# Attention rewritten: a maxima-only rows pass, softmax sums by matmuls of ones, sixteen half-groups over a ring of five score banks

## What is computed

```python
q = (query @ Wq).reshape(bsz, tgt_len, 2 * H, D)      # H = 16, D = 16; k alike, v: H heads of 2 * D
q = apply_rotary_emb = apply_rotary_interleaved(q, cos, sin)
q1, q2 = (q[:, :, :, 0], q[:, :, :, 1])
attn1 = causal_attn_pair(q1, k1, v1, v2, mask, scale)  # softmax(q1 k1^T) v, float32
attn2 = causal_attn_pair(q2, k2, v1, v2, mask, scale)
f1 = jnp.fft.rfft(attn1, axis=1)
f2 = jnp.fft.rfft(attn2, axis=1)
attn_freq = f1 - lambda_full * f2
attn_freq = attn_freq * filt[None, :, None, None]
attn = jnp.fft.irfft(attn_freq, n=tgt_len, axis=1)
attn = attn * jax.lax.rsqrt(jnp.mean(attn * attn, axis=-1, keepdims=True) + EPS) * rms_weight
return attn.reshape(bsz, tgt_len, H * 2 * D) @ Wout
```

## Time and profile before

| | |
|---|---|
| time, median of 3 runs | 1559.61 us (1551.4 to 1561.73) |
| the profiled execution, span | 1553.8 us |
| normalise and what leads to attention's first scores | 0 to 133 us |
| attention, first 16 rows units alone | 133 to 171.7 us |
| attention, rows and probs together, to the last values | 171.7 to about 1014 us |
| end of attention, start of `middle` | 1014 to 1098 us |
| `middle` and `last` | 1098 to 1553 us |
| busy over the span | PE 1252.6, DVE 855.8, ACT 809.2, POOL 590.6 us |

### The profile page before, as it was taken

The page is one execution under the profiler, slowest core; times in us unless marked ns, Lnnn a source line. Parts: engine busy times, 40 slices in busy tenths (PEclk is TensorE's granted clock), DMA queues, the critical chain, the costliest instruction groups (busy, mean ns, idle before and its releaser), DMA issues. The chain is left out here.

```text
span 1553.8 us, 21592 instructions
## 1 busy us (share of the span) xinstructions
PE 1252.6 (81%) x6637; PEld 639.4 (41%) x6652; DVE 855.8 (55%) x1502; ACT 809.2 (52%) x1741; POOL 590.6 (38%) x662
## 2 busy tenths in 40 slices
PE   6854898798897897898998888956798888775985
PEld 4622233333443433334334323324566555542543
DVE  6554544834835635635636438145777655542886
ACT  2304577877887876877877888822121111110211
POOL 4433407146244252262361301200566655672121
PEclk9985789989899898998899799887999998997998
DMA  4364711802604505306207002013122111113330
GB/s 144 117 139 73 117 16 42 109 16 68 84 16 86 68 35 94 40 35 101 32 34 116 17 22 89 16 36 102 62 81 69 62 62 48 41 41 100 110 107 36
DMA packets 69358, 104.16 MB, mean 67 GB/s; under 512 B 8448, under 2 KB 34688, under 8 KB 69248
## 3 DMA queue, kind: packets, MB, share of 16 engines
q1 hardware_dynamic: 57472, 69.26, 22.9%
q0 software_dynamic: 7168, 25.17, 4.5%
q10 hardware_dynamic: 4608, 8.39, 1.4%
HBM read 68.85 MB, written 33.95 MB: 66 GB/s over the span
## 5 line engine op out<-in xcount | busy, mean ns | idle before, releaser
L1058 ACT ACTIVATE score<-score,nmax 128x1024 f32<-128x1024 f32 (+7 forms) x512 | 364.8, 713 | 165.7 <-DVE nmax L934 83.8
L1088 ACT ACTIVATE prob<-score 128x1024 f32<-128x1024 f32 (+3 forms) x384 | 297.7, 812 | 39.7 <-PE score L795 24.4
L776 PE MATMUL score<-kst,qst 96*128 96x512 bf16 (+3 forms) x768 | 222.8, 370 | 93.1 <-ACT score L1058 73.2
L937 DVE TENSOR_REDUCE nmax<-score 128x1 f32<-128x640 f32 (+3 forms) x256 | 250.7, 1020 | 80.3 <-PE score L780 77.4
L934 DVE TENSOR_REDUCE nmax<-score 128x2 f32<-128x256 f32 (+3 forms) x128 | 105.3, 825 | 243.5 <-PE score L780 243.5
L791 PE MATMUL score<-qst,kst 99*128 99x512 bf16 (+3 forms) x768 | 217.9, 354 | 24.4 <-ACT score L1058 10.3
L720 PE MATMUL misc<-xnT,wg 128*128 128x512 f32 x256 | 139.6, 644 | 24.4 <-DVE raw L874 16.7
L776 PEld LDWEIGHTS score<-kst,qst 96*128 96x128 bf16 x768 | 64.3, 104 | 219.9 <-ACT score L1058 143.7
L791 PEld LDWEIGHTS score<-qst,kst 99*128 99x128 bf16 x768 | 74.3, 103 | 191.6 <-ACT prob L1088 67.7
L780 PE MATMUL score<-mask_s,identb 128*128 128x128 bf16 x512 | 117.1, 238 | 0.0
L1131 POOL TENSOR_TENSOR sq<-y 128x512 f32<-128x512 f32 x14 | 14.5, 1034 | 255.5 <-DVE y L897 196.0
(11 more groups left out here) (229 smaller groups left out, 2168.2 us busy)
## 6 DMA issues: line engine op xcount, KB each, us to landing
piece_scratch<-pieces POOLq DMA_DIRECT2D x16, 768.0 KB, 4.1
qst<-piece_scratch SPq DMA_DIRECT2D x48, 256.0 KB, 9.6
kst<-piece_scratch SPq DMA_DIRECT2D x48, 256.0 KB, 18.9
x1in<-in_query SPq DMA_DIRECT2D x16, 256.0 KB, 2.7
v_scratch<-v ACTq DMA_DIRECT2D x16, 256.0 KB, 2.0
vg<-v_scratch SPq DMA_DIRECT2D x8, 512.0 KB, 15.7
att_scratch<-y SPq DMA_DIRECT2D x8, 512.0 KB, 2.7
m_aT<-att_scratch SPq DMA_DIRECT2D x16, 256.0 KB, 2.9
```

The source lines that it names most:

```text
L776: mm = nc.tensor.matmul(score[slot][:, bank, 0:w], qst[0:PIECES, g.slot, pair + k, i * P:(i + 1) * P], kst[0:PIECES, g.slot, pair + k, c0: ...
L937: nc.vector.tensor_reduce(nmax[:, pair, i:i + 1], src[:].rearrange("p a b -> p (a b)")[:, 0:(i + 1) * P], AX.X, ALU.max, negate=True).then ...
L1058: ins = nc.scalar.activation(s, s, ACT.Exp, bias=nmax[:, pair + k, i:i + 1], accum_out=den[:, pair + k, i:i + 1])
L1088: nc.scalar.activation(prob[:, u % NPROB, :, t0:HALF], score[slot][:, :, t0:HALF], ACT.Exp).then_inc(s_exp, 1)
```

## The change

**Half-groups.** The 8 groups of 8 pairs become 16 sets of 4 (one map of 4 heads each, `SETS`); `qst` and `kst` hold four sets. `stack` issues 12 transfers of half the size per set.

**Rows pass.** A unit now fills one bank of 512 columns. There are 38 per set. Short ones hold 4 or 2 heads with one mask matmul over all. DVE takes the maxima (L839 in the new file, 608 reduces in all, 384 before); ACT does nothing in this pass, and a rows unit gives back its bank after the maximum. For queries 512 and up a row's maxima come in two parts, joined by one minimum. The shift is the maximum alone, in two bfloat16 pieces: a probs matmul has 98 rows.

**Probs pass and sums.** A probs unit is one head in one bank: 768 exps of up to 512 columns instead of 384 of up to 1024. For every `values` event PE now also multiplies the same probabilities by `ones` into a new bank `den`, 4 more float32 matmuls. So there are 192 events as before, each of 8 float32 matmuls instead of 4. After each half ACT turns `den` into its reciprocal (Ln, then Exp with scale -1, `norm`), and DVE multiplies `acc` by it (`output`); in odd sets it also multiplies by minus lambda and adds to `oT`. POOL no longer scales the values.

**Order and waits.** One written-out list (`schedule`) with no hardware loop: the 38 rows units of set 0 stand alone, then each set's 48 probs units are merged with the next set's rows units; the last set's stand alone. `values` stands four units behind its probs, `norm` three units later and `out` six. The score ring has five single banks. The first values of a half wait for `norm`'s first read of `den` and for `out` to have read `acc`. The work on `misc` (projections, low-pass, shift transposes) is otherwise the same.

```diff
+SETS = 2 * B * G
+RING = 5
+NPROB = 12
+PROD = 6 * D
+ROWS = PROD + 2
...
+        for c0 in range(0, (i + 1) * P, HALF):
+            width = min(HALF, (i + 1) * P - c0)
+            n = max(1, HALF // width) if width != 384 else 1
+            units += [(i, c0, width, h, n) for h in range(0, GH, n)]
...
-    return [(h, j, w, g) for h in range(2) for j in range((h + 1) * TB // 2) for w in range(2) for g in (0, 2)]
...
+    return [(h, j, head) for h in range(2) for j in range((h + 1) * TB // 2) for head in range(GH)]
...
+def schedule():
+    units, start = [], []
+    units += [("rows", 0, u) for u in range(NRU)]
+    for n in range(SETS):
+        start.append(len(units))
+        mine = [("probs", n, m) for m in range(NPU)]
+        ahead = [("rows", n + 1, u) for u in range(NRU)] if n + 1 < SETS else []
+        units += merge(mine, ahead)
+    start.append(len(units))
...
+        for v in range(NV):
+            k = at["probs", n, v * GH + GH - 1] + VALUES_LATER
+            put(k, ("values", n, v))
+            if v in (NV // 3 - 1, NV - 1):
+                h = int(v == NV - 1)
+                put(k + NORM_LATER, ("norm", n, h))
+                put(k + OUT_LATER, ("out", n, h))
...
-        score = [ctx.enter_context(nc.psum_tensor(f"score{i}", [P, 2, HALF], F32)) for i in range(NSLOT)]
+        score = [ctx.enter_context(nc.psum_tensor(f"score{i}", [P, HALF], F32)) for i in range(RING)]
         acc = ctx.enter_context(nc.psum_tensor("acc", [P, HALF], F32))
+        den = ctx.enter_context(nc.psum_tensor("den", [P, HALF], F32))
         misc = ctx.enter_context(nc.psum_tensor("misc", [P, HALF], F32))
         miscb = misc[:].bitcast(BF16)
...
+            def slot_free(k):
+                if k >= RING:
+                    kind, count = done[k - RING]
+                    pe.wait_ge(s_max if kind == "rows" else s_exp, count)
...
+            def rows(n, u):
+                i, c0, width, first, heads = RU[u]
+                k = place["rows", n, u]
+                slot_free(k)
+                bank = score[k % RING][:, 0:heads * width].rearrange("p (a s) -> p a s", a=heads)
+                for x in range(heads):
+                    mm = nc.tensor.matmul(bank[:, x], qst[0:PROD, n % 4, first + x, i * P:(i + 1) * P],
+                                          kst[0:PROD, n % 4, first + x, c0:c0 + width], start=(x == 0),
+                                          stop=(x == heads - 1), skip_group_check=True)
+                if c0 + width == (i + 1) * P:
+                    mask = mask_s[:].rearrange("p (o s) -> p o s", o=1).broadcast_to([P, heads, P])
+                    mm = nc.tensor.matmul(bank[:, :, width - P:width], identb[:], mask, start=False, stop=True,
+                                          skip_group_check=True)
+                mm.then_inc(s_unit, 1)
...
-            def values(g, m):
...
-                if j == 0 and which == 0:
-                    if g.reg is not None or g.c > 0 or h:
-                        pe.wait_ge(s_oT, g.times(2, h))
-                end = j == (h + 1) * TB // 2 - 1 and which == 1
-                for head in range(GH):
-                    pslot = (m - 1 + head // 2) % NPROB
-                    v = (vg, vn)[which]
-                    mm = nc.tensor.matmul(acc[head * 32:head * 32 + 32, t0:HALF],
-                                          v[:, g.slot, j, head * 32:head * 32 + 32],
-                                          prob[:, pslot, head % 2, t0:HALF],
-                                          start=(j == 0 and which == 0), stop=end, skip_group_check=True)
+            def values(n, v):
+                h, j, _ = PU[v * GH]
+                pe.wait_ge(s_exp, probs_done(n, v * GH + GH - 1))
                 t0 = max(j * P - h * HALF, 0)
+                if j == 0 and 2 * n + h > 0:
+                    pe.wait_ge(s_den, 2 * n + h)
+                    pe.wait_ge(s_acc, 2 * n + h)
+                end = j == (h + 1) * TB // 2 - 1
+                for total, bank in enumerate((acc, den)):
+                    for head in range(GH):
+                        x = slice(head * 2 * D, (head + 1) * 2 * D)
+                        mm = nc.tensor.matmul(bank[x, t0:HALF], ones[:] if total else vg[:, n // 2 % 2, j, x],
+                                              prob[:, (n * NPU + v * GH + head) % NPROB, t0:HALF],
+                                              start=(j == 0), stop=end, skip_group_check=True)
                 mm.then_inc(s_pv, 1)
...
+            def maxima(n, u):
+                i, c0, width, first, heads = RU[u]
+                k = place["rows", n, u]
+                dve.wait_ge(s_unit, k + 1)
+                dst = nm0[:, i] if i < TB // 2 else (nm2 if c0 else nm1)[:, i - TB // 2]
+                nc.vector.tensor_reduce(dst[:, first:first + heads].rearrange("p (a o) -> p a o", o=1),
+                                        score[k % RING][:, 0:heads * width].rearrange("p (a s) -> p a s", a=heads),
+                                        AX.X, ALU.max, negate=True).then_inc(s_max, 1)
...
-            def output(g, h):
-                dve.wait_ge(s_pv, g.times(NV, (NV // 3, NV)[h]))
-                nc.vector.tensor_copy(oT[:, h * HALF:(h + 1) * HALF], acc[:]).then_inc(s_oT, 1)
+            def output(n, h):
+                g, q = n // 2, 2 * n + h
+                dve.wait_ge(s_rden, q + 1)
+                if n % 2 == 0:
+                    nc.vector.tensor_tensor(oT[:, half(h)], acc[:], rden[:, q % 2], ALU.mult).then_inc(s_acc, 1)
                 else:
+                    if n > 1 or h:
+                        dve.wait_ge(s_oT, 2 * g + h)
+                    nc.vector.scalar_tensor_tensor(second[:], acc[:], nlam[:], rden[:, q % 2], ALU.mult, ALU.mult)\
+                        .then_inc(s_acc, 1)
+                    dve.wait_ge(s_acc, q + 1)
+                    nc.vector.tensor_tensor(oT[:, half(h)], oT[:, half(h)], second[:], ALU.add).then_inc(s_oT, 1)
...
-            def sums(u, maxed, slot):
-                i, pair, cnt = RU[u]
-                act.wait_ge(s_max, maxed)
-                src = score[slot]
-                for k in range(cnt):
-                    s = src[:, k, 0:(i + 1) * P] if cnt == 2 else src[:].rearrange("p a b -> p (a b)")[:, 0:(i + 1) * P]
-                    ins = nc.scalar.activation(s, s, ACT.Exp, bias=nmax[:, pair + k, i:i + 1],
-                                               accum_out=den[:, pair + k, i:i + 1])
-                ins.then_inc(s_exp, 1)
...
+            def norm(n, h):
+                q = 2 * n + h
+                act.wait_ge(s_pv, NV * n + (NV if h else NV // 3))
+                if q >= 2:
+                    act.wait_ge(s_acc, q - 1)
+                nc.scalar.activation(rden[:, q % 2], den[:], ACT.Ln).then_inc(s_den, 1)
+                act.wait_ge(s_den, q + 1)
+                nc.scalar.activation(rden[:, q % 2], rden[:, q % 2], ACT.Exp, scale=-1.0).then_inc(s_rden, 1)
```

More of the change, by code:

```diff
@@ L482, in attention @@
+    order = {name: k + 1 for k, name in enumerate(uses)}
+    opened = None
+    for e in EVENTS:
+        if e[0] in ("part", "use"):
+            assert opened in (None, e[1]), (opened, e)
+            opened = e[1] if e[0] == "part" else None
+    place = {u: k for k, u in enumerate(UNITS)}
+    seen = {"rows": 0, "probs": 0}
+    done = []
+    for kind, _, _ in UNITS:
+        seen[kind] += 1
+        done.append((kind, seen[kind]))
     with ExitStack() as ctx:
@@ L1000, in _ @@
[L1000 to L1011 removed]
+            begun = 0
@@ new lines, in _ @@
+            for kind, x, u in EVENTS:
+                if kind == "probs":
+                    h, j, head = PU[u]
+                    k, p = place["probs", x, u], x * NPU + u
+                    act.wait_ge(s_unit, k + 1)
+                    if p >= NPROB:
+                        act.wait_ge(s_pv, (p - NPROB) // GH + 1)
+                    t0 = max(j * P - h * HALF, 0)
+                    nc.scalar.activation(prob[:, p % NPROB, t0:HALF], score[k % RING][:, t0:HALF], ACT.Exp)\
+                        .then_inc(s_exp, 1)
+                elif kind == "norm":
+                    norm(x, u)
+                elif kind == "root":
+                    root(x, u)
```

779 lines of the change are left out of this document (304 added, 475 removed).

## The result

The changed kernel took 1600.01 us, median of 4 runs (1598.15 to 1601.5), the kernel before 1556.78 in the runs beside it (1551.4 to 1561.73). The ratio is 1.0281, 95% interval 1.0258 to 1.0304: **2.8% slower**, 43 us. The profiled execution took 1599.38 with a span of 1597.8. Attention's last values event ends at 1060.4 us, where it ended at 1014; what stands behind it takes 537 us, and took 540.

A forecast was written before the change was run, and what follows sets the result against it. PE and ACT were taken to hold each other in attention. Start 156, PE's work 753, border waits 48, clock 40, other losses 58 and end 3 gave 1058 against 1014, 43 us slower: 1603 us, range 1540 to 1665.

The forecast's parts named there:

- The losses: PE from first probs unit to last values event: 48 us border waits, 40 clock, 58 small waits and weight loads.
- One sign of being right: PE's busy time over the kernel was to go up by 100 to 150 us.
- The start: First scores at 127.5 us, then set 0's 38 rows units alone, bound by DVE; first probs at 156 us.
- The sums: Four more float32 matmuls per values event: double event 1.90 us at 512 columns, between 1.86 and 2.00.
- PE's sum 753: PE's work from first probs unit to last values event: 753 us, 121 more than before.
- ACT and DVE: In attention ACT ends near 415 of 860 us and bounds only single waits; DVE's added work is mostly hidden.
- The border waits: At each half's border PE's next values event waits behind norm and output: 23 of 1.75 and 8 of 0.9, 48 us.
- The clock: Ten falls to half clock in 31 half borders, some 4 us of work lost per fall: 40 us.
- The other losses: In attention, 20 us for DVE bursts and values awaiting the last exp, 38 us for weight loads not hidden.
- come out even: Rival: attention loses 87 to 118 us, with shorter border waits and few falls; 1559.6 within 15; chance 0.2.
- Full clock and packing: Rival: in attention PE stays at full clock and packs; loss 77 us, time 1534 us; chance 0.15.
- The ring: Rival: in attention the ring of five score banks becomes the bound; 1727 us, with half of that 1665; chance 0.15.

The follow-up runs named there:

- e2: Changed kernel with the sums' matmuls kept only for each half's first key block, 160 of 192 sum events left out: 1532.76 us, ratio 0.9868.
- e3: Kernel before with every values matmul issued a second time into acc, ACT keeping its exps for sums: 1636.74 us, ratio 1.0539.
- e5: Changed kernel with norm one unit behind a half's last values instead of three, and out three instead of six: 1563.71 us, ratio 1.0039.
- e1: Changed kernel with only the projections moved, to 34, 39, 52, 59 units, away from DVE's making of the shift's pieces: 1559.99 us, ratio 1.0029.
- e9: Changed kernel with norm 1 and out 3 units behind the last values, projections at 28, 35, 45, 52, values still at four units: 1516.06 us.
- e10: Changed kernel with norm directly behind the last values, out 2 units, pieces' transposes 7 instead of 5, projections at 28, 35, 45, 52: 1503.91 us.
- e4: Changed kernel with four score banks instead of five: 1617.4 us, ratio 1.0406.
- e6: Changed kernel with norm 1 and out 3 units behind, and each half's first values four units later, the second two later: 1596.6 us.
- e8: Changed kernel with norm 1, out 3, projections at 28, 35, 45, 52, values six units behind, a half's first two three and one more: 1572.67 us.

## Why the prediction was right, point by point

**The sign and the size** came from the right place: 1600.0 measured, 1603 predicted, and attention's end at 1060.4 instead of 1058. The losses were right in their sum, 146 us taken and 154 measured, and not in their parts, as the points below say. One sign of being right did not come: PE's busy time was to rise by 100 to 150 us and rose by 73.5, presumably since matmuls at half clock are longer in the profile and PE spent less time there than before.

**The start.** First scores at 126.1 (127.5 predicted), first probs at 153.6 (156). Both terms held; key stacks of half the size end PE's first wait 7 us sooner than 132.95.

**The sums.** 1.86, 1.42, 1.00 and 0.58 us for the double events, where 1.90, 1.47, 1.05 and 0.62 were taken between a lower bound of 1.86 and 2.00. The entry is paid once, so the lower bound was the value; it makes PE's sum 753 some 8 us too high. By the Trainium skill, TensorEngine Tiling (Array Packing), section Key Properties, the engine drains where the tiling mode changes; the trace agrees, with 0.14 us at the change and none between the two fours. e2 and e3 confirm the term: the end moves with the matmuls, by 67 of 96 us and 82 of 124.

**ACT and DVE.** ACT is busy 395 us in the merged stretch, 415 was predicted, and it is no bound. DVE stands idle 287 us ahead of its maxima.

**The border waits.** 48 us predicted, 41.9 measured, 31 waits, 29 of them of 0.8 to 1.7 us. The chain of Ln, Exp and product stands in the trace as it was worked out, and e5 gets 29 of the 41.9 back by moving it. Not in the working: 8 of the waits, 13.7 us, end on an exp for these values that stands behind Ln and Exp on ACT.

**The clock: the size held, the reason did not.** 40 us were put down to ten falls at the borders. There were 16, at about 2.5 us each and not 4, and 12 of them come with the wait for the pieces. The total is 41 us by the table. It stands by luck: the place, the number and the price of a fall were all different. What held is the direction: the fuller PE lost 41 us to the clock where it lost 67 before (66 in the prediction's estimate).

**The other losses** hid what was missed. 58 us were taken for weight loads and small waits; in the trace 36 are the wait for the pieces, and 906.8 - 753 - 42 - 36 - 40 leaves about 36 for all else, of which some 18 are other idle time of PE and 18 work or short stalls above the prices. The step that failed is the one that sized DVE's bursts by their lengths in the kernel before: there the pieces took 0.19 to 0.30 us, once 0.46, and never stood beside more than the last 0.2 us of a POOL product. The prediction asked whether POOL is waited for and answered no, which is so. It did not ask whether POOL would hold DVE. e1 shows the price: 40 us, as much as the whole loss against the kernel before. Without this collision the change would have come out even (1.0029), which had a chance of 0.2.

**The rivals.** Full clock and packing needs both waits gone: e9 and e10 are that kernel, with 1516 and 1504 us, at half clock for 24 and 22 us. The ring is not the bound (e4), but it becomes one where values stand later (e6, e8).

## What to carry to other kernels

Work moved onto the fullest engine costs most of its price even when that engine was 19% idle: two thirds of each added microsecond came through, in both directions. Much of the missing third is the clock, which fell less when PE had more to do (152 us at half before, 91 with the work added) and more when it had less (99 us in the changed kernel, 123 with few sums). After a rewrite of the order, look first for small instructions whose longest time is many times the median (176 and 2268 ns here) and ask which engine runs beside them; moving four numbers in the order gave back 40 us. Put a hand-over at a buffer's end as early as its input allows, and do not delay its consumer. e6 and e8 lost 33 and 44 us by it; as argued there, the delay takes from another engine the time that it got behind the long events.

## What the runs showed of the hardware

A DVE instruction that takes 0.17 us alone, on 16 columns in SBUF, took 1.91 and 2.26 us beside POOL products of 2.33, and ended with the product that ran when it began; both the one with two SBUF inputs (L823) and the float32 to bfloat16 copy with one (L822) did so. A larger one with two SBUF inputs was held too: L854, 0.69 us alone on 512 columns, took 2.50 to 2.58 three times beside POOL's last instruction of a rotation. Maxima read from PSUM kept their 0.66 to 0.69, and so did the product of a PSUM and an SBUF input (L851, 0.74 to 0.75 with and without POOL beside it). The Trainium skill, GPSIMD Engine Reference, section Specifications, says that GpSimd shares its SBUF interfaces with VectorE, with contention for DVE instructions with two SBUF inputs or in a 2-port mode. The trace agrees for L823 and gives the size; in which mode the copy of L822 ran, no row shows.

The clock fell from its full level (2.4 GHz) to half of it (1.2 GHz) after single waits of PE of 1.6 to 3.9 us. It did not fall every time: of seven waits of 1.65 us ahead of `acc` in the changed kernel three had a fall behind them. A wait so costs more than its own length: e1 took 22 us of idle time away and 8 of 16 falls, and won 40.
